# Global attention with row maxima taken one and a half heads ahead, and the products with the inverses as one GpSimd operation for each pair of heads

## The reference

```python
k = jnp.repeat(k, GROUPS, axis=1); v = jnp.repeat(v, GROUPS, axis=1)
attn = jnp.einsum('bhqd,bhkd->bhqk', q, k) / math.sqrt(HD)
attn = attn + slopes[None, :, None, None] * rel[None, None, :, :]
attn = jax.nn.softmax(attn, axis=-1)
out = jnp.einsum('bhqk,bhkd->bhqd', attn, v)
return out.transpose(0, 2, 1, 3).reshape(b, l, H * HD) @ Wo
```

## Time and profile before

| | us |
|---|---|
| runs | 1157.36, 1158.15, 1158.62 |
| profiled execution, its time | 1160.06 |
| profiled execution, its span | 1158.3 |
| TensorE busy in the span | 1078.5 (93%) |
| VectorE busy | 901.1 (78%) |
| GpSimd busy | 721.4 (62%) |
| ScalarE busy | 637.0 (55%) |
| TensorE idle ahead of weight loads L892, until VectorE's maximum | 93.6 |
| VectorE's maxima L825, 256 of them | 312.5 |
| VectorE's quarter divisions L849, 64 of them | 80.8 |

### The profile page before, as it was taken

The page is one execution under the profiler, slowest core; times in us unless marked ns, Lnnn a source line. Parts: engine busy times, 40 slices in busy tenths (PEclk is TensorE's granted clock), DMA queues, the critical chain, the costliest instruction groups (busy, mean ns, idle before and its releaser), DMA issues. The chain is left out here.

```text
span 1158.3 us, 23136 instructions
## 1 busy us (share of the span) xinstructions
PE 1078.5 (93%) x8352; PEld 664.7 (57%) x8352; DVE 901.1 (78%) x1586; ACT 637.0 (55%) x1000; POOL 721.4 (62%) x526
## 2 busy tenths in 40 slices
PE   6884899999999999999999999769999898999988
PEld 4452454555555455455555545736777795777678
DVE  6995767777877788777887765669999589888867
ACT  2442365566666556665666664036666455666544
POOL 3662266657666665666666576699986337666526
PEclk8996699999999999999999999969999999999999
DMA  8899421514235133342243100201111100111101
GB/s 256 273 278 346 95 65 38 119 43 107 52 68 120 38 87 71 74 105 53 68 90 74 38 20 20 92 9 30 33 34 41 26 2 19 32 32 33 39 19 36
DMA packets 83457, 89.03 MB, mean 77 GB/s; under 512 B 32740, under 2 KB 66064, under 8 KB 83344
## 3 DMA queue, kind: packets, MB, share of 16 engines
q1 hardware_dynamic: 83344, 87.55, 30.1%
HBM read 53.57 MB, written 24.25 MB: 67 GB/s over the span
## 5 line engine op out<-in xcount | busy, mean ns | idle before, releaser
L825 DVE CUSTOM_DVE_ANT_0 junk<-psum,alibi 128x1024 bf16<-128x1024 f32 x256 | 312.5, 1221 | 135.0 <-PE psum L892 126.0
L797 ACT ACTIVATE E<-psum,keybias_sb 128x1024 f32<-128x1024 f32 x256 | 274.8, 1113 | 179.4 <-PE psum L916 166.2
L734 POOL TENSOR_TENSOR xpos_sb<-xpos_sb,E 128x1024 f32<-128x1024 f32 x96 | 231.3, 2409 | 128.0 <-ACT E L797 123.5
L928 PE MATMUL psum<-E,V 128*64 128x512 f32 x1024 | 248.7, 607 | 0.0
L892 PE MATMUL psum<-KH,QH 64*128 64x512 f32 x512 | 121.4, 470 | 15.2 <-DVE M L825 7.6
L928 PEld LDWEIGHTS psum<-E,V 128*64 128x64 f32 x1024 | 62.2, 136 | 117.7 <-issue 111.8
L738 POOL TENSOR_TENSOR xpos_sb<-xpos_sb 128x1024 f32<-128x1024 f32 x32 | 76.1, 2377 | 69.3 <-DVE xpos_sb L835 69.3
L892 PEld LDWEIGHTS psum<-KH,QH 64*128 64x128 f32 x512 | 49.8, 191 | 110.3 <-DVE M L825 93.6
L916 PE MATMUL psum<-QH,KH 64*128 64x512 f32 x512 | 102.4, 396 | 0.7 <-DVE M L825 0.7
L916 PE MATMUL psum<-QL,KH 64*128 64x512 f32 x512 | 101.6, 392 | 0.0
L916 PE MATMUL psum<-QH,KL 64*128 64x512 f32 x512 | 101.4, 392 | 0.0
(11 more groups left out here) (148 smaller groups left out, 2057.2 us busy)
## 6 DMA issues: line engine op xcount, KB each, us to landing
QH<-qa_scratch SPq DMA_DIRECT2D x64, 256.0 KB, 4.7
qa_scratch<-tH SPq DMA_DIRECT2D x8, 1024.0 KB, 5.5
qa_scratch<-tL SPq DMA_DIRECT2D x8, 1024.0 KB, 7.8
QL<-qa_scratch SPq DMA_DIRECT2D x64, 128.0 KB, 4.9
XF<-inverse_scratch SPq DMA_DIRECT2D x32, 256.0 KB, 3.6
vp_att<-v_att SPq DMA_DIRECT2D x64, 128.0 KB, 2.3
KH<-k_scratch SPq DMA_DIRECT2D x16, 256.0 KB, 3.9
KL<-k_scratch SPq DMA_DIRECT2D x16, 256.0 KB, 5.1
```

Of the source, the lines that this page charges most:

```text
L734: pool.tensor_tensor(sum_p[:, s, :], first, E[:, k % 4, :], ALU.add)\
L797: act.activation(E[:, k % 4, :], scores(k % 2), ACT.Exp, bias=kb).then_inc(exp_done, 1)
L825: dve.tensor_tensor_reduce(junk[:, :], banks(max_bank(i, k), 2), alibi[:, s, :], -1.0, BIG, ALU.add, ALU.min, M[:, s, k:k + 1]).then_inc(m ...
L928: last = pe.matmul(banks(6 + i % 2)[HD * ch:HD * ch + HD, :], V[:, g, k, :], E[:, k % 4, ch * 512:(ch + 1) * 512], start=(k == 0), stop=(k ...
```

## The change

- The maxima lead by 12 steps (`LEAD`) instead of 16: 12 of them ahead of head 0, and step k of head i does maximum number 8 i + k + 12. The first scores wait for maxima 11 and 12 instead of 14 and 15.
- TensorE's small products stand in the pair k = 4, between the maximum and the products with V. ScalarE takes maxima and denominators before exponential 6, the maxima first.
- `spread_inverse` is cut in two. `spread_denominators` stays last in SyncE's head. `widen_inverse`, the store and the broadcast of head i - 2, stands ahead of `load_m`. VectorE inverts head i - 2 at k = 3 of head i.
- The division is one GpSimd operation over all 1024 columns, in even heads from 4 on, after GpSimd's second step of summing (the one with exponential 2). The last two pairs are divided after the last head, with the four `second_rstd` between them.

```diff
+            LEAD = TB + TB // 2
+            def max_ahead(i, k):
+                return divmod(TB * i + k + LEAD, TB)
...
+                    def widen_inverse(i, s):
                         need(sp, inv_done, i + 1)
                         need(sp, inv_in, 16 * (i - 1))
                         sp.dma_start(inv_d[s].rearrange("(p e) -> p e", e=TB), inv8[:, s, :]).then_inc(inv_out, 16)
                         need(sp, inv_out, 16 * (i + 1))
-                        need(sp, o_done, QUARTERS * (i // 2))
+                        need(sp, o_done, i // 2)
                         sp.dma_start(inv_wide[HD * s:HD * s + HD, :], inv_d[s].partition_broadcast(HD)).then_inc(inv_in, 16)
...
+                        if i > 1:
+                            widen_inverse(i - 2, i % 2)
                         if i + 1 < HEADS:
                             load_m(i + 1, (i + 1) % 2)
                         if i > 0:
-                            spread_inverse(i - 1, (i - 1) % 2)
+                            spread_denominators(i - 1, (i - 1) % 2)
...
-                    spread_inverse(HEADS - 1, (HEADS - 1) % 2)
+                    widen_inverse(HEADS - 2, HEADS % 2)
+                    spread_denominators(HEADS - 1, (HEADS - 1) % 2)
+                    widen_inverse(HEADS - 1, (HEADS - 1) % 2)
...
+                    def divide(j):
+                        need(pool, inv_in, 32 * (j + 1))
+                        need(pool, o_taken, 4 * (j + 1))
+                        o = OT[:, j // PAIRS, j % PAIRS, :, :].rearrange("p t c -> p (t c)")
+                        pool.tensor_tensor(o, o, inv_wide, ALU.mult).then_inc(o_done, 1)
...
+                            if n == 1 and i >= 4 and i % 2 == 0:
+                                divide((i - 4) // 2)
...
+                    divide(HEADS // 2 - 2)
                     for t in range(EARLY):
                         second_rstd(pool, t)
+                    divide(HEADS // 2 - 1)
...
-                            if k == 4 and i > 0:
+                            if k == 6 and i + 1 < HEADS:
+                                take_m(i + 1, (i + 1) % 2)
+                            if k == 6 and i > 0:
                                 take_denominators(i - 1)
-                            if k == 4 and i + 1 < HEADS:
-                                take_m(i + 1, (i + 1) % 2)
...
-                            if 1 <= k <= QUARTERS and i % 2 == 1 and i > 1:
-                                divide((i - 3) // 2, k - 1)
-                            if k == 6 and i > 0:
-                                invert(i - 1, (i - 1) % 2)
+                            if k == 3 and i > 1:
+                                invert(i - 2, i % 2)
...
-                            pe.wait_ge(max_done, 2 * TB - 2 + k)
+                            pe.wait_ge(max_done, LEAD - 1 + k)
...
+                            if k == 4:
+                                small_products(i)
                             if k > 0:
                                 pv_step(i, k - 1)
                             elif i > 0:
                                 pv_step(i - 1, TB - 1)
                             pv_step(i, k)
-                            if k == 2:
-                                small_products(i)
```

More of the change, by code:

```diff
@@ L684, in load_m, with spread_denominators @@
                                          mrow[TB // 2 * ch:TB // 2 * (ch + 1), s, :].bitcast(F32)).then_inc(ld_m[s], 16)
[L686 removed]
+                    def spread_denominators(i, s):
                         need(sp, den_taken, i + 1)
@@ L817, in _, with max_step @@
                 def _(dve):
-                    def max_step(i, s, k):
+                    def max_step(i, k):
+                        s = i % 2
                         need(dve, max_mm, TB * i + k + 1)
@@ L854, in head @@
                                 sum_step(i - 1, (i - 1) % 2, 1)
-                            if i + 2 < HEADS:
-                                max_step(i + 2, i % 2, k)
-                            if 1 <= k <= QUARTERS and i % 2 == 1 and i > 1:
-                                divide((i - 3) // 2, k - 1)
-                            if k == 6 and i > 0:
-                                invert(i - 1, (i - 1) % 2)
+                            if max_ahead(i, k)[0] < HEADS:
+                                max_step(*max_ahead(i, k))
+                            if k == 3 and i > 1:
+                                invert(i - 2, i % 2)
                             if k == 5:
                                 sum_step(i, i % 2, 0)
-                    for i in range(2):
-                        for k in range(TB):
-                            max_step(i, i, k)
+                    for n in range(LEAD):
+                        max_step(*divmod(n, TB))
                     need_landed(dve, 1)
@@ L870, in _ @@
                     sum_step(HEADS - 1, (HEADS - 1) % 2, 1)
+                    invert(HEADS - 2, HEADS % 2)
                     invert(HEADS - 1, (HEADS - 1) % 2)
@@ L874, in _ @@
                         residual(dve, t)
-                    for n in range(QUARTERS):
-                        divide(HEADS // 2 - 1, n)
                 @block.tensor
@@ L886, in max_step @@
                             need(pe, mrow_done, 1 if i >= 2 else 0)
-                        need(pe, max_done, TB * i + k - (2 if i < 2 else 0))
+                        need(pe, max_done, TB * i + k - (2 if TB * i + k < LEAD else 0))
                         for ch in range(2):
@@ L952, in head @@
                             qk_step(i, k + 1)
-                            if i + 2 < HEADS:
-                                max_step(i + 2, k)
+                            if max_ahead(i, k)[0] < HEADS:
+                                max_step(*max_ahead(i, k))
+                            if k == 4:
+                                small_products(i)
                             if k > 0:
@@ L959, in head @@
                             pv_step(i, k)
-                            if k == 2:
-                                small_products(i)
-                            if i + 2 < HEADS:
-                                max_step(i + 2, k + 1)
-                    for i in range(2):
-                        for k in range(TB):
-                            max_step(i, k)
-                            if (i, k) == (1, 2):
-                                turn_m(0, 0)
+                            if max_ahead(i, k + 1)[0] < HEADS:
+                                max_step(*max_ahead(i, k + 1))
+                    for n in range(LEAD):
+                        max_step(*divmod(n, TB))
+                        if n == TB + 2:
+                            turn_m(0, 0)
                     for i in range(HEADS):
@@ L977, in _ @@
                     pe.wait_ge(exp_done, TB * HEADS)
-                    pe.wait_ge(o_done, QUARTERS * PAIRS)
+                    pe.wait_ge(o_done, PAIRS)
                     for t in range(2):
```

9 lines of the change are left out of this document (1 added, 8 removed).

## The result

The median of the changed kernel is 1159.72 us (13 runs, 1158.80 to 1161.51), that of the kernel before in the same comparison 1158.27 (13 runs, 1156.53 to 1159.58). The ratio is 1.0015, interval 1.0008 to 1.0022: slower by 1.45 us where 1.0 us faster was forecast. The profiled execution took 1159.72 us with a span of 1157.9.

The account below looks back on a forecast made before the run. TensorE was taken to bound the heads, VectorE's maxima the start, SyncE's transfer chain the end. -4.1 + 1.0 - 4.6 + 0 + 4.0 + 2.7 = -1.0 us, from 1158.15 to 1157.1; range 1153.0 to 1162.0.

Parts of the forecast that it names:

- Ahead of head 0: Start of attention: first scores wait for maximum 11 instead of 14, -4.1 us, or -3.6 if QM is late.
- Four maxima in head 30: Head 30: the four maxima moved from the start now stand in TensorE's full stream, 0.25 us each, +1.0 us.
- Divisions off VectorE: Odd heads: without VectorE's quarter divisions they last as long as even ones, -4.6 us.
- It can't be more: Odd heads: taking the divisions off VectorE can gain no more than the 4.6 us surplus.
- The division on GpSimd: Even heads: it ends just before VectorE's sum, cost 0; up to 0.45 us too long costs nothing.
- The small products moved: Each head, behind the fifth maximum: same instructions, cost 0, bounds 0.05 us a head (1.5 us) either way.
- The QM wait: Ends of heads 4, 8, 12, 16, 20, 24: 0.5 us for five, 1.5 in head 16, +4.0 us, bounds 1.3 to 9.3.
- QM is only behind part of the broadcast: Late heads: the reason for taking 0.5 us for five heads, near the lower end of 0.3 to 1.3.
- The end: After the last head: denominators fetched 1.7 us later, last division 1.0 longer on GpSimd, block end +2.7 us.
- The clock: Rival, after the last head: 3.3 us idle lowers TensorE's clock, next projections lose 2.9 us, 1160.0; chance 0.14.
- QM in time: Rival, head starts: QM never late, so +4.0 becomes 0, 1153.1 us; chance 0.27.
- the long queue: Rival, behind the loads: five heads stall 1.7 us, head 16 4.2, 12.7 instead of 4.0, 1165.8; chance 0.12.

Follow-up runs that it names:

- the longer division: Changed kernel with load_m ahead of widen_inverse, plus a GpSimd memset of an unused tile right behind the division in even heads: 1154.86 us.
- the two kernels with more waits: Changed kernel with 24, or 8, long-satisfied waits added on TensorE ahead of the attention block: 1160.24 us with 24, 1159.64 us with 8.
- QM ahead: Changed kernel with load_m moved ahead of widen_inverse again on SyncE: 1155.3 us, ratio 0.9971 to the kernel before.
- the end's order: Changed kernel with the last denominators spread before head 30's inverses are widened, and the last pair divided on VectorE in one operation: 1158.81 us.
- both repairs: Changed kernel with load_m ahead of widen_inverse, last denominators spread before head 30's widening, and last pair divided on VectorE: 1152.39 us, ratio 0.9952.

## Why the prediction was wrong

The waits were foreseen where they came; two terms of the sum were too low, and together they turned a small gain into a small loss. By its steps:

**Ahead of head 0: right.** -4.1 forecast and measured. As foreseen, QM was not what came late: TensorE waited for VectorE's M there.

**Four maxima in head 30: right.** +1.0 forecast, +0.9 measured.

**Divisions off VectorE: right here, for a reason only half seen.** -4.6 forecast and measured, and the kernel with this part alone gives it too (-4.7). The fourteen odd heads at 0.29 make only 4.1 of it. The other 0.5 is head 17, which lasted 19.09 us before and was not read apart; in it VectorE also waited for the broadcast, behind the denominators of head 16 that came late themselves:

```profile
449.04 1.70 DVE L849 TENSOR_TENSOR OT<-OT,XF 128x256 f32<-128x256 f32 x1 [0.54 <-DMA XF<-inverse_scratch]
```

Whether that wait is all of the 0.5 was not tried; with the GpSimd division alone head 17 takes 18.29 too. But "It can't be more" held only against the kernel before: in the new order, quarters on VectorE cost 1.18 us in each even head.

**The division on GpSimd: right, with the room underrated.** Zero was forecast with 0.45 us in hand. Head 8 after:

```profile
279.33 2.39 POOL L753 TENSOR_TENSOR xpos_sb<-xpos_sb,E 128x1024 f32<-128x1024 f32 x1
281.67 2.39 POOL L743 TENSOR_TENSOR OT<-OT,XF 128x1024 f32<-128x1024 f32 x1
284.01 2.39 POOL L753 TENSOR_TENSOR xpos_sb<-xpos_sb,E 128x1024 f32<-128x1024 f32 x1
...
286.87 1.22 DVE L859 TENSOR_TENSOR xpos_sb<-E 128x1024 f32<-128x1024 f32 x1
```

The three operations start every 2.34 us, so they end at 286.40, 0.47 us ahead of VectorE's sum instead of 0.15. With the longer division 0.95 us more was nearly free.

**The small products moved: right.** Plain heads are 18.29 us, no longer than before.

**The QM wait: right in kind and place, 1.5 us too low.** The six heads were named, and the chain (loads, store, broadcast, QM). What failed is the size, 2.5 us for five heads: it was read from head 8 alone, where the store would have landed, and the broadcast been issued, 291.8 - 276.58 = 15.2 us into the head. In the kernel after, the store took 5.1 to 5.9 us to land, and the broadcast was issued 15.57, 15.42, 15.67, 15.90, 16.26 and 15.69 us into heads 4, 8, 12, 16, 20 and 24. Head 8 itself lost 0.4 us, close to the 0.5 taken for it; heads 4, 12, 20 and 24 lost 0.7, 0.8, 1.3 and 0.9, together 4.0 for the five instead of 2.5. Head 16, singled out for 1.5 us, lost 0.9. The excess over 18.29 is 4.9 in the six heads, and 0.6 more in the heads behind them, where the first score product after the wait starts late; the prediction didn't have that.

The ground given for 0.5, that "QM is only behind part of the broadcast", was wrong too, though it cost little, since the broadcast took the lower end of its forecast of 3.3 to 4.4 us. In head 8 it was issued at 287.02, and landed after

```profile
DMA to landing us min/median/max: 3.3/3.3/3.3
```

at 290.3; TensorE's first scores of head 9, waiting for a QM that was issued 0.5 to 1.2 us later, start at 290.31. In the transfers of the six heads the broadcast lands 18.90, 18.71, 19.01, 19.19, 19.53 and 19.11 us into the head, and the next head begins at 18.95, 18.71, 19.11, 19.18, 19.55 and 19.17: never more than 0.1 apart. QM's semaphore says the same. Its last update came 1.64 to 1.69 us after the issue of the second transfer in the heads where the broadcast had been issued 1.5 us ahead of the first, and 2.0 to 2.2 us after it in the six late heads, within 0.06 us of the broadcast's landing. The rule that the prediction cited from the Trainium skill (DMA: Bandwidth & Descriptors, Queues, rings and completion order), that a semaphore lands only after the engine's earlier writes, agrees with these rows. By them the rule makes about half of the stall, 0.3 to 0.55 us a head. With 1.65 us for QM and the same issue times, about 2.4 of the 4.9 us would be left (an estimate from these rows; no kernel put QM between the store and the broadcast): that half is the late issue alone.

**The end: +3.4 instead of +2.7.** The delay of the denominators (1.6 against 1.7) and the longer division (0.9 against 1.0) were there, each 0.1 shorter. What the sum lacks is the last store, 2.8 us to landing instead of 1.4, and the last broadcast, 3.5 instead of 4.1: together +0.8. The store's 1.4 us come from the packet of the instruction queue that it now meets, as the rows and the two kernels with more waits showed. Why the last broadcast took 4.1 us before and 3.5 now is open. TensorE's idle of 4.03 us is the 3.3 that were foreseen and this 0.7. The step that failed is the silent one, that the transfers at the end keep their own times.

**The clock: the event came, its price didn't.** The rival said that the idle would bring the clock down and cost 2.9 us. It fell, which the prediction had named as a sign of being wrong: 0.60 on average in the first 4.2 us of the projections, 16.16 us for them instead of 14.53. But the kernel after reaches the next stage no later than the kernel before:

```profile
755.23 0.47 PE L1409 MATMUL psum<-ident,XF 128*128 128x128 f32 x1 [6.67 <-POOL XF L619]
```

is 22.83 us after its block start, and before

```profile
755.05 0.48 PE L1398 MATMUL psum<-ident,XF 128*128 128x128 f32 x1 [8.44 <-POOL XF L619]
```

is 22.97. TensorE waits for GpSimd there, 6.67 us now and 8.44 before. GpSimd's chain begins when its inputs have landed and runs from this row on, through eight such operations with two short ones between each two of them, until 752.9:

```profile
741.36 0.73 POOL L557 TENSOR_TENSOR xpos_sb<-xpos_sb,scale_row 128x256 f32<-128x256 f32 x1 [2.67 <-DMA xpos_sb<-in_xpos_dram]
```

The rival's price, half of the slow stretch, needed a TensorE bound behind the block, and no row of before was read for that. That the rival's time, 1160.0, lies 0.3 us from the measured median is luck: its cost was nothing here. Its argument also counted the idle of the earlier trace rows as 5.5 us; the clock was down 3.5 us into it.

**The sum.** -4.1 + 0.9 - 4.6 + 5.5 + 3.4 = +1.1 us against the forecast -1.0: of the 2.1 between them the QM term accounts for 1.5, the end for 0.7, and head 30 for -0.1. Of the rivals, QM in time and the long queue fall with the six rows: the stalls were 0.4 to 1.3 us, 0.8 on average, between the two.

**What stays open.** QM ahead is worth 5.6 us over the heads in the profiled executions and 4.4 in the medians; the whole change +1.1 in the rows of the table, -0.4 in the span, and +1.45 in the medians; the end's order 1.65 and 0.9. The medians of a kernel's runs have a spread of 1 us and more, so differences of some tenths can't be placed. Nor can the single heads: with the waits added, the six late heads lasted 18.48 to 19.46 and 18.63 to 19.63 us in another order (head 16 18.74 and 18.63, head 24 19.46 and 19.63), with sums of 4.7 and 5.1 over 18.29 against 4.9. Why a single head loses 0.4 or 1.3 was not settled.

## What to carry to other kernels

A small transfer issued just behind a large one is costed at the large one's landing, and what the issuing engine waits for ahead of it is added first, from the rows of every place where it happens and not of one. The order on the issuing queue is a choice that can be free: what the bottleneck engine waits for goes ahead of what only a side engine waits for. A part of a change is tried alone on the kernel before: here one part gave 4 us and the rest gave it back. And before a lower clock is priced, the rows behind it say whether that engine is what the next stage waits for.

## What the runs showed of the hardware

- Two QM transfers of one row each, issued 0.5 to 1.2 us behind the 256 KB broadcast of the inverses, landed with it, within 0.06 us in all six heads, 2.0 to 2.2 us after the second one's issue; with the broadcast 1.5 us ahead the second took 1.64 to 1.69. The store of a head's inverses took 1.4 us to land with nothing ahead of it, 2.6 when issued 1.3 us behind a broadcast (3.3 and 3.0 when issued 0.6 us behind one, with a packet of the instruction queue beside them), 5.1 to 5.9 behind a group's loads of keys, values and queries.
- Beside one packet of 16 KB on the instruction queue, 0.9 to 1.4 us long, a 4 KB store took 2.3 to 3.0 us instead of 1.4, in eight traces. It landed 1.0 to 1.2 us after the packet's end; in the kernel after, the last nine of its 144 small packets came just when that packet was through (725.11).
- GpSimd operations of 128x1024 that follow each other with nothing to wait for start every 2.34 us, though each is shown at 2.39.
- VectorE's sum of 1.22 us took 1.53 where its first 0.45 us lay beside the end of a GpSimd sum, and a quarter division took 2.15 beside one. The Trainium skill (SBUF — State Buffer, Who interferes with whom) has the two excluding each other; these rows agree.
- An idle of 4.03 us at the end was followed by 3.4 us of TensorE at half clock (1.2 GHz), one of 2.65 us (both repairs) too (0.65 over the first 3.7 us of the projections, which took 16.16), one of 2.38 us (the order at the end) by none.
